# Routed rows of an expert layer: pads written once instead of cleared storage, one array for both parts, 20 + 19 tiles instead of 31 + 15, and a new order of the work

## The chip, the cores and the metric

The kernel runs on one core of a Trainium2 chip. The metric is device time in microseconds (us): the median of several executions, and one execution that the hardware profiler recorded. TensorE is called PE, VectorE DVE, ScalarE ACT, GpSimd POOL and SyncE SP, as in the profile.

## The reference

A batch is 128 rows of 128 numbers; there are 32 batches. Everything is float32.

```python
x = x + attn(layernorm(x))                       # 16 heads of 8, full 128x128 scores, w_out, x added again
x = x + xattn(layernorm(x), ctx, ctx)            # 16 heads of 64, rotary q and k, a row sees itself and 32 before it
# expert layer, on n = layernorm(x):
idx = argmax(n @ router.T)                       # one of 8 experts for each row
y  = (silu(n @ gate[idx].T) * (n @ up[idx].T)) @ down[idx].T
ys = (silu(n @ w_gate_s.T) * (n @ w_up_s.T)) @ w_down_s.T      # shared expert, all rows
x = x + n + y + ys
```

Which expert a row goes to is known only on the chip.

## The kernel before

Each engine runs a list of steps, written out by hand in one loop `for s in range(PERIODS)`. `batch(f, s - k)` runs step `f` for batch `s - k`, so a **period** `s` holds one batch of every step, each for another batch: `a_*` (norm, q/k/v), `b_*` (self attention), `c_v`, `r_k`, `r_q`, `d_*` (cross attention), `e_*`/`f_*` (router, shared expert, scatter). The order within a period, the lags `k`, and the table `BANK`, which puts every PE result into one of 8 PSUM banks, were fixed together. `take` makes PE wait until the last user of a bank has released it. `WARM` lists matmuls on ones that fill PE's waits in the first periods.

The routed expert is done afterwards, on rows that have been sorted by expert:

- `f_pos(b)`: PE counts rows by expert so far and gives each row of batch `b` its place in a DRAM array `z_xs`; DVE picks it (`psf`), POOL turns it into an integer. `f_send(b)` on POOL scatters the 128 rows (normed row, number of the row, and the sum to which the expert's result is added: 272 floats) with an indirect DMA.
- The batches are in two chunks, `CHUNKS = [24, 8]`, each with its own array. An expert's region has room for all rows of the chunk. So that unused rows of a tile do no harm, `clear(b)` on SP writes `fill` rows over the whole region, a part for each batch: one DMA of 8 x 128 rows, 1088 KB, in every period, and one more of the same size per chunk for a tile that belongs to nobody.
- After the last batch of a chunk DVE works out in `tile_table` which rows and which expert each of the chunk's tiles has: 24 + 7 = 31 tiles of 128 rows, and 8 + 7 = 15. This is the most that can be needed, since every expert's last tile may be part full.
- A tile: `load_r` (SP) loads 128 rows; `x_tr` (PE, line 399) turns them; `x_up` (410) gate and up; tanh on ACT, `x_gate` on DVE; `x_hT` (419); `x_dn` (425, 427); `x_y` adds on DVE; `x_send` (POOL, 1023) scatters the result to the output. `tile(f, s - k, i)` puts four tiles in each late period of the loop, for the first chunk only; the second chunk's tiles run after the loop (`last`).

PE's steps with the lines that the profile names: `b_s` 207, `b_nm` 216, `b_st` 224/228, `b_pv` 239, `c_v` 272, `r_k` 282, `r_q` 292, `d_s` 299/307, `d_t` 320, `d_pv` 334/337, `d_wo` 348, `f_up` 366, `f_pos` 385 to 389.

Of the kernel before, what the change touches and what calls it, by code (L numbers as in the profile page):

```python
# [13 lines left out]
NB = 32  # L14
# [3 lines left out]
CHUNKS = [24, 8]  # L18
TILES = [n + 7 for n in CHUNKS]
NT = sum(TILES)  # L20
# [10 lines left out]
BANK = dict(a=5, cnt=2, dn=5, ds0=0, ds1=3, ds2=1, ds3=4, dt0=1, dt1=4, dt2=2, dt3=4, et=5, gu=0, hi0=0, hi1=1, kE=7,  # L31
            kO=0, ln=1, lo0=6, lo1=4, nmt=5, oT=5, po=5, pos=6, qE=3, qO=7, qkv=6, rt=3, s0=6, s1=2, s2=5, s3=7,
            st0=6, st1=2, st2=5, st3=7, v0=3, v1=4, wo=2, x1=7, xg0=3, xg1=7, xg2=3, xg3=2, xgt0=1, xgt1=2, xgt2=3,
            xr0=5, xr1=0, xr2=5, xr3=6, xrt0=4, xrt1=5, xt0=1, xt1=6, xt2=7, xt3=2, xtt0=0, xy0=6, xy1=0, xy2=2,
            xy3=1, xyt0=6, xyt1=7)
WARM = {('a', 0): 36, ('nmt', 0): 43, ('st0', 0): 9, ('po', 0): 33, ('oT', 0): 13, ('qE', 0): 9, ('st0', 1): 16,
        ('ds0', 0): 14, ('oT', 1): 28, ('lo1', 0): 17}
S0, PERIODS = 24, 42


SEMS = """d_c1 d_cb d_c2 d_wk d_wv d_wq d_wo d_we d_ex d_tab
# [10 lines left out]
            d_x=3, d_cx=4, d_zf=4, d_ze=2, d_sc=4, d_xr=12, d_out=4)  # L52


def build(nc, A):
    ctx = ExitStack()
    with ctx:
# [13 lines left out]
        cb = sb("cb", [128, 1336], U16)  # L71
# [15 lines left out]
        cnt = sb("cnt", [128, 48])  # L87
        cmpb = sb("cmpb", [128, 8 * MOST])
        exf = sb("exf", [128, 2 * MOST])
# [46 lines left out]
        ecap = cb[:, 768:784].bitcast(BF16).rearrange("p (c e) -> p c e", c=2)  # L136
        far, eye = cb[:, 784:1296].bitcast(BF16).rearrange("p (w q) -> p w q", w=4), cb[:, 1296:1328].bitcast(BF16)
        iota = cb[:, 1328:1336].bitcast(BF16)
        woutT, bo, fill, tri = c2[:, 0:128], c2[:, 128:256], c2[:, 256:256 + ROW], c2[:, 528:592]
        tri = tri.rearrange("p (a b) -> p a b", a=8)  # L140
        rtT, ids = c2[:, 592:600], c2[:, 608:640].bitcast(U32)
# [31 lines left out]
        def _(pe):  # L173
# [205 lines left out]
            def f_pos(b):  # L379
                first = b == FIRST[chunk(b)]  # L380
                last = b + 1 in (FIRST[1], NB)
                p = take("pos", b, (S["v_cnt"], chunk(b) + 1) if last else (S["v_pse"], b + 1))
                pe.wait_ge(S["v_oh"], b + 1)
                pe.wait_ge(S["p_acc"], b + 1)
                pe.matmul(p[:, 0:8], ones[:, :], ecap[:, chunk(b), :], start=True, stop=False, skip_group_check=True)
                if not first:
# [43 lines left out]
            for s in range(PERIODS):  # L430
                batch(b_s, s - 3)
                tile(x_up, s - 31, 0)
                tile(x_dn, s - 32, 1)
                tile(x_hT, s - 32, 3)
                batch(c_v, s - 3, 1)
                batch(b_ln, s - 4)
                tile(x_dn, s - 32, 2)
                tile(x_tr, s - 31, 2)
                batch(d_pv, s - 5, 0)
                batch(r_q, s - 4, 0)  # L440
                batch(e_tr, s - 6)
                batch(r_q, s - 4, 1)
                batch(d_t, s - 5, 1)
                batch(b_nm, s - 3)
                tile(x_dn, s - 32, 3)
                batch(f_pos, s - 7)
                batch(f_up, s - 6)
                batch(d_pv, s - 5, 1)
                batch(b_st, s - 3)
                batch(d_s, s - 4)  # L450
                tile(x_hT, s - 31, 0)
                tile(x_tr, s - 31, 3)
                tile(x_up, s - 31, 1)
                batch(b_pv, s - 3)
                batch(d_wo, s - 5)
                batch(b_oT, s - 3)
                tile(x_dn, s - 31, 0)
                tile(x_up, s - 31, 2)
                batch(r_k, s - 2, 0)
                batch(a_qkv, s - 2)  # L460
                batch(b_cn, s - 3)
                batch(f_dn, s - 6)
                tile(x_tr, s - 30, 0)
                tile(x_hT, s - 31, 1)
                batch(c_v, s - 2, 0)
                batch(b_x1, s - 3)
                batch(a_tr, s - 1)
                tile(x_up, s - 31, 3)
                tile(x_tr, s - 30, 1)
                tile(x_hT, s - 31, 2)  # L470
                batch(r_k, s - 2, 1)
                batch(d_t, s - 4, 0)
# [7 lines left out]
        def _(dve):  # L480
# [148 lines left out]
            def f_pos(b):  # L629
# [6 lines left out]
                dve.tensor_reduce(f[:, 8:9], f[:, 0:8], AX.X, ALU.add).then_inc(S["v_pse"], 1)  # L636
                if b + 1 in (FIRST[1], NB):
                    dve.tensor_copy(cnt[:, 0:8], bank("pos")[:, 8:16]).then_inc(S["v_cnt"], 1)
                    tile_table(chunk(b))


            def tile_table(c):
                n, t0, T = CHUNKS[c], TILE0[c], TILES[c]
# [3 lines left out]
                                  steps[:, 0:n].rearrange("p (a j) -> p a j", a=1).to_broadcast([128, NE, n]),  # L647
                                  ALU.is_gt).then_inc(S["v_own"], 1)
                dve.wait_ge(S["v_own"], own())
                dve.tensor_reduce(cnt[:, 8:16], cm, AX.X, ALU.add).then_inc(S["v_own"], 1)  # L650
                c2 = cmpb[:, 0:64].rearrange("p (e f) -> p e f", e=NE)
                dve.wait_ge(S["v_own"], own())
                dve.tensor_tensor(c2, cnt[:, 8:16].rearrange("p (a f) -> p a f", a=1).to_broadcast([128, NE, NE]),
                                  tri[:, :, :], ALU.mult).then_inc(S["v_own"], 1)
                dve.wait_ge(S["v_own"], own())
                dve.tensor_reduce(cnt[:, 16:24], c2, AX.X, ALU.add).then_inc(S["v_own"], 1)
                c3 = cmpb[:, 0:8 * T].rearrange("p (j e) -> p j e", e=NE)
                dve.wait_ge(S["v_own"], own())
                dve.tensor_tensor(c3, cnt[:, 16:24].rearrange("p (a e) -> p a e", a=1).to_broadcast([128, T, NE]),
                                  tiles[:, 0:T].rearrange("p (j a) -> p j a", a=1).to_broadcast([128, T, NE]),  # L660
                                  ALU.is_le).then_inc(S["v_own"], 1)
                dve.wait_ge(S["v_own"], own())
                dve.tensor_reduce(exf[:, 0:T], c3, AX.X, ALU.add).then_inc(S["v_own"], 1)
                dve.tensor_scalar(cnt[:, 24:32], cnt[:, 8:16], -1.0, float(n), ALU.mult, ALU.add).then_inc(S["v_own"], 1)
# [3 lines left out]
                dve.tensor_tensor(c3, c3, cnt[:, 24:32].rearrange("p (a e) -> p a e", a=1).to_broadcast([128, T, NE]),  # L668
# [7 lines left out]
                dve.wait_ge(S["v_own"], own())  # L676
                dve.tensor_scalar(exr[:, t0:t0 + T], exf[:, MOST:MOST + T], 128.0, None, ALU.mult).then_inc(S["v_ex"], 1)
# [17 lines left out]
            for s in range(PERIODS):  # L695
                batch(d_ri, s - 6, 3)
                tile(x_gate, s - 33, 3)
                batch(r_k3, s - 4)
                batch(b_max, s - 4, 0)
                batch(b_max, s - 4, 3)  # L700
                batch(b_max, s - 4, 1)
                tile(x_y, s - 33, 1)
                tile(x_gate, s - 32, 0)
                batch(b_max, s - 4, 2)
                tile(x_y, s - 33, 2)
                batch(d_ox, s - 6, 0)
                batch(r_q1, s - 5)
                batch(r_q3, s - 5)
                batch(f_pos, s - 8)
                tile(x_y, s - 33, 3)  # L710
                batch(f_route, s - 7)
                batch(f_gate, s - 7)
                batch(d_ox, s - 6, 1)
                batch(d_max, s - 5, 1)
                batch(a_stats, s - 1)
                batch(d_max, s - 5, 3)
                batch(d_max, s - 5, 0)
                batch(d_ri, s - 5, 1)
# [18 lines left out]
        def _(act):  # L737
# [142 lines left out]
            for s in range(PERIODS):  # L880
                batch(b_ps, s - 5, 1)
                batch(b_ps, s - 5, 3)
                batch(b_ps, s - 5, 2)
                tile(x_hT, s - 33, 0)
                tile(x_xT, s - 33, 3)
                batch(d_exp, s - 6, 1)
                tile(x_th, s - 33, 1)
                batch(b_oT, s - 5)
                batch(d_exp, s - 6, 0)
                batch(d_exp, s - 6, 2)  # L890
                tile(x_th, s - 33, 2)
                batch(a_q, s - 4)
                batch(b_cnT, s - 5)
                batch(d_exp, s - 6, 3)
                batch(a_aT, s - 3)
                tile(x_xT, s - 32, 0)
# [168 lines left out]
        def _(sp):  # L1065
# [14 lines left out]
            def clear(b):  # L1080
                c, k = chunk(b), b - FIRST[chunk(b)]
                Z = A["z_xs"][c].rearrange("(t p) d -> p t d", p=128)
                if b == 0:
                    sp.wait_ge(S["d_c2"], 16)
# [129 lines left out]
```

## Time and profile before

| | us |
|---|---|
| median of 3 runs | 826.36 (820.38 to 828.25) |
| the profiled execution, device time | 820.7 |
| its span, first to last instruction | 818.7 |
| PE busy | 754.7 |
| DVE, ACT, POOL busy | 556.5, 542.3, 534.4 |

Busy time shows which engine has least room. A row of the timeline gives start, duration, engine, line, operation and, in brackets, the idle time just before it with what ended it. In the chain of waits "issue" stands where the engine waited for nothing that the profile shows.

### The profile page before, as it was taken

How to read it: one execution, taken by the hardware profiler on the slowest of the kernel's cores; microseconds unless marked ns; L12 is line 12 of the kernel's file. 1: busy time of each engine (PE TensorE's matmuls, PEld its weight loads, DVE VectorE, ACT ScalarE, POOL GpSimd, SP SyncE). 2: the span in 40 equal slices, each digit the busy share in tenths (PEclk: the TensorE clock that was granted, in tenths of full speed). 3: DMA queues.
4: the chain of work that ended last, by engine and by line, in shares of the span. 5: the costliest groups of instructions: out<-in, count | busy, mean ns of one | idle time of the engine just before them, and what ended most of it. 6: DMA issues, size and time to landing. Idle time of an engine off the chain costs nothing.

```text
span 818.7 us, 31875 instructions
## 1 busy us (share of the span) xinstructions
PE 754.7 (92%) x11894; PEld 615.7 (75%) x11894; DVE 556.5 (68%) x1414; ACT 542.3 (66%) x1964; POOL 534.4 (65%) x864
## 2 busy tenths in 40 slices
PE   6888999999999999989999999999869999999794
PEld 5666888887887888877787888888657778877453
DVE  3465777776777777756777777777677776665542
ACT  2366777776777777755777777777547677666242
POOL 4365677777667777766666777777546567676624
PEclk9999999999999999999999999999989999999888
DMA  6003122222222222222211122122134213321130
GB/s 228 10 12 111 64 90 91 92 90 83 89 90 90 70 71 70 70 70 70 70 64 68 67 75 70 67 75 85 53 121 146 67 48 91 103 87 59 42 109 13
DMA packets 56805, 64.29 MB, mean 79 GB/s; under 512 B 4014, under 2 KB 52916, under 8 KB 56656
## 3 DMA queue, kind: packets, MB, share of 16 engines
q1 hardware_dynamic: 52928, 54.06, 20.3%
q0 software_dynamic: 3008, 6.57, 2.3%
q8 instruction: 99, 1.62, 0.8%
q10 hardware_dynamic: 720, 1.63, 0.5%
q14 instruction: 50, 0.41, 0.2%
HBM read 17.80 MB, written 45.35 MB: 77 GB/s over the span
## 4 chain that ended last, share of the span: by engine, by line
PE 88%; issue 4%; DVE 3%; DMA 2%; ACT 1%; SPq 1%; POOL 0%; POOLq 0%; DVEq 0%; ACTq 0%
PE P L307 8%; PE P L348 8%; PE P L292 7%; PE P L272 7%; PE P L282 7%; PE P L320 5%; PE P L410 5%; PE P L334 4%; PE P L239 4%; PE P L224 4%; PE P L207 4%; PE P L366 4%; PE P L247 2%; PE P L337 2%; PE P L374 2%
## 5 line engine op out<-in xcount | busy, mean ns | idle before, releaser
L820 ACT ACTIVATE PX<-P,mx 128x128 f32<-128x128 f32 x512 | 183.1, 409 | 59.7 <-DVE mx L582 59.7
L582 DVE TENSOR_REDUCE mx<-P 128x4 f32<-128x512 f32 x128 | 83.1, 673 | 111.9 <-PE P L307 111.9
L990 POOL TENSOR_TENSOR PX<-PX,mx 128x512 f32<-128x512 f32 x128 | 131.9, 1040 | 3.6 <-DVE mx L587 2.6
L820 ACT ACTIVATION_READ_ACCUMULATOR PX<-P,mx 128x1 f32 x512 | 128.0, 250 | 0.0
L829 ACT ACTIVATE PT<-P 128x512 f32<-128x512 f32 x128 | 69.6, 596 | 45.2 <-PE P L320 44.5
L985 POOL TENSOR_TENSOR rq<-rq,tq 128x1024 f32<-128x1024 f32 x32 | 75.4, 2358 | 34.5 <-DVE tq L546 34.5
L307 PE MATMUL P<-rk,rq 32*128 32x128 f32 x2048 | 73.7, 286 | 18.2 <-issue 18.1
L936 POOL TENSOR_SCALAR st<-st 128x1 f32<-128x1 f32 x96 | 22.0, 229 | 103.4 <-DVE st L490 100.3
L521 DVE TENSOR_REDUCE nmf<-P 128x4 f32<-128x512 f32 x128 | 79.8, 683 | 13.7 <-PE P L207 13.7
L307 PEld LDWEIGHTS P<-rk,rq 32*128 32x128 f32 x2048 | 66.9, 196 | 20.2 <-issue 20.0
L784 ACT ACTIVATE PS<-P 128x512 f32<-128x512 f32 x128 | 66.1, 603 | 22.7 <-PE P L228 22.7
L980 POOL TENSOR_TENSOR rk<-rk,tk 128x1024 f32<-128x1024 f32 x32 | 75.6, 2363 | 0.9
L272 PE MATMUL P<-wvT,cxT 128*128 128x512 f32 x128 | 68.9, 620 | 0.1
L292 PE MATMUL P<-cT,wq 128*128 128x128 f32 x512 | 68.9, 281 | 0.0
L282 PE MATMUL P<-cxT,wk 128*128 128x128 f32 x512 | 68.6, 277 | 0.0
L1023 POOL DMA_INDIRECT out<-yst,xrow x46 | 45.8, 995 | 34.4 <-DVE yst L692 22.2
L348 PE MATMUL P<-woT,oX 128*128 128x128 f32 x512 | 65.6, 281 | 0.0
L348 PEld LDWEIGHTS P<-woT,oX 128*128 128x128 f32 x512 | 59.6, 191 | 7.4 <-issue 6.1
L292 PEld LDWEIGHTS P<-cT,wq 128*128 128x128 f32 x512 | 61.9, 191 | 3.7
L282 PEld LDWEIGHTS P<-cxT,wk 128*128 128x128 f32 x512 | 63.2, 194 | 1.8 <-issue 1.7
L938 POOL TENSOR_TENSOR st<-st,nhalf 128x1 f32<-128x1 f32 x96 | 54.6, 569 | 8.0
L334 PE MATMUL P<-PT,V 64*64 64x96 f32 x1024 | 56.2, 249 | 0.0
(148 smaller groups left out, 1884.9 us busy)
## 6 DMA issues: line engine op xcount, KB each, us to landing
z_xs<-c SPq DMA_DIRECT2D x34, 1088.0 KB, 5.1
xrow<-z_xs SPq DMA_DIRECT2D x46, 136.0 KB, 2.1
ew<-in_ew SPq DMA_DIRECT2D x9, 384.0 KB, 3.4
x<-in_x SPq DMA_DIRECT2D x32, 64.0 KB, 1.9
cxT<-in_ctxT SPq DMA_DIRECT2D x31, 64.0 KB, 1.8
out<-yst,xrow POOLq DMA_INDIRECT x46, 2.2
wk<-in_wk SPq DMA_DIRECT2D x1, 512.0 KB, 4.2
wvT<-in_wvT SPq DMA_DIRECT2D x1, 512.0 KB, 6.9
```

The source lines that it names most:

```text
L272: pe.matmul(p, cxT[b % 4][:, :], wvT[:, 4 * half:4 * half + 4, :].rearrange("p a n -> p (a n)"), start=True, stop=True).then_inc(S[f"t_v{h ...
L282: t = pe.matmul(p[:, c * 128:c * 128 + 128], wk[:, e, c, :], cxT[b % 4][:, :], start=True, stop=True)
L292: t = pe.matmul(p[:, c * 128:c * 128 + 128], wq[:, e, c, :], cT[b % 2][:, :], start=True, stop=True)
L307: t = pe.matmul(p[r][:, c * 128:c * 128 + 128], rq[b % 2][32 * r:32 * r + 32, e, c, :], rk[b % 2][32 * r:32 * r + 32, e, c, :], start=Fals ...
L334: pe.matmul(lo[64 * u:64 * u + 64, 96 * q:96 * q + 96], V[b % 3][0:64, 8 * k + 2 * q + u, :], PT[(2 * b + k) % 3][0:64, 2 * q + u, 0:96], ...
L348: t = pe.matmul(p[:, 0:128], oX[2 * (b % 2) + k][:, q, :], woT[:, 4 * k + q, :], start=(k == 0 and q == 0), stop=(k == 1 and q == 3))
L521: dve.tensor_reduce(nmf[b % 2][:, 0, r, :], v3(bank(f"s{r}")), AX.X, ALU.max, negate=True).then_inc(S["v_bm"][r], 1)
L582: dve.tensor_reduce(mx[b % 3][:, 0, r, :], v3(bank(f"ds{r}")), AX.X, ALU.max, negate=True).then_inc(S["v_dm"][r], 1)
L820: t = act.activation(PX[(4 * b + r) % 6][:, c, :], p[:, c * 128:c * 128 + 128], ACT.Exp, bias=m[:, 0, r, c:c + 1], scale=1.0, accum_out=m[ ...
L980: pool.tensor_tensor(rk[b % 2][:, :, :, :], rk[b % 2][:, :, :, :], tk[:, :, :, :], ALU.add).then_inc(S["p_k"], 1)
L985: pool.tensor_tensor(rq[b % 2][:, :, :, :], rq[b % 2][:, :, :, :], tq[:, :, :, :], ALU.add).then_inc(S["p_q"], 1)
L990: pool.tensor_tensor(X[:, :, :], X[:, :, :], mx[b % 3][:, 2, r, :].rearrange("p (h a) -> p h a", a=1).to_broadcast([128, 4, 128]), ALU.mul ...
```

## The change

Both chunks now share one array `z_xs` with `CAP = 33` tiles of room for each expert. Chunks are 27 and 5 batches. At the first table only **full** tiles are taken: 27 batches hold at least 20 of them whatever the routing, so `TILES[0] = 27 - 7 = 20`; what is over stays in the array for the second table, which takes the rest of 39: 19 tiles. The running counts are no longer restarted at the second chunk. A part full tile exists only at the end of each expert's rows, so `clear` is gone. `pads`, once, when batch 30 is counted, writes 256 `fill` rows behind the rows counted so far for each of the 8 experts (8 DMAs of 272 KB, each at an address that SP loads from `padr`); the scatter of batch 31 waits for them (`d_pad`). `nobody` writes 8 tiles of 136 KB, one in each of periods 18 to 25.

Orders, lags, `BANK` and `WARM` (218 matmuls before, 185 now) are all new. Tiles start in period 35 instead of 30, `PERIODS` is 45 instead of 42.

```diff
-CHUNKS = [24, 8]
-TILES = [n + 7 for n in CHUNKS]
-NT = sum(TILES)
+CHUNKS = [27, NB - 27]
+CAP = NB + 1
+NT = NB + 7
+TILES = [CHUNKS[0] - 7, NT - CHUNKS[0] + 7]
...
 # DVE, f_pos
+                if b == NB - 2:
+                    dve.scalar_tensor_tensor(out=padr[:, :], in0=experts, scalar=float(128 * CAP), in1=bank("pos")[:, 8:16],
+                                             op0=ALU.mult, op1=ALU.add).then_inc(S["v_pad"], 1)
...
 # DVE, tile_table
+                if c == 1:
+                    dve.tensor_tensor(own_tiles, own_tiles, done, ALU.subtract).then_inc(S["v_own"], 1)
...
+                if c == 0:
+                    dve.memset(cnt[:, 40:41], 0.0).then_inc(S["v_own"], 1)
+                    dve.tensor_scalar(upto, incl, float(T), None, ALU.min).then_inc(S["v_own"], 1)
...
+                    dve.tensor_tensor(done, upto, before, ALU.subtract).then_inc(S["v_own"], 1)
+                else:
+                    dve.tensor_tensor(w, w, after, ALU.add).then_inc(S["v_own"], 1)
...
+                    dve.tensor_tensor(w, w, done, ALU.subtract).then_inc(S["v_own"], 1)
...
 # POOL, f_send
-                pool.wait_ge(S["d_zf"][b % 4], 16 * (b // 4 + 1))
+                if b == NB - 1:
+                    pool.wait_ge(S["d_pad"], 16 * NE)
...
 # SP
-            def clear(b):
...
-                sp.dma_start(Z[:, k:NE * CHUNKS[c]:CHUNKS[c], :], fill[:, :].rearrange(
-                    "p (a d) -> p a d", a=1).to_broadcast([128, NE, ROW])).then_inc(S["d_zf"][b % 4], 16)
+            def pads(b):
+                if b == NB - 2:
+                    sp.wait_ge(S["v_pad"], 1)
+                    for e in range(NE):
+                        row = sp.value_load(padr[0:1, e:e + 1], min_val=128 * CAP * e, max_val=128 * (CAP * e + CAP - 2))
+                        sp.dma_start(A["z_xs"][bass.ds(row, 256), :].rearrange("(t p) d -> p t d", p=128),
+                                     empty.to_broadcast([128, 2, ROW])).then_inc(S["d_pad"], 16)
+            def nobody(s):
+                e = s - 18
+                if 0 <= e < NE:
+                    k = 128 * (NE * CAP + e)
+                    sp.dma_start(A["z_xs"][k:k + 128, :], fill).then_inc(S["d_ze"], 16)
...
 # the order, two lines of each kind
-                batch(f_pos, s - 8)
...
+                batch(f_pos, s - 7)
...
-                tile(x_up, s - 31, 0)
...
+                tile(x_up, s - 35, 0)
```

Four places show how instructions moved. First SP, in two periods near the end of the first chunk; `z_xs<-c` is a clear, `cxT` and `x` are the loads of a batch.

```order
97 L1090 DMA z_xs<-c 128x8x272
98 L1077 DMA cxT<-in_ctxT 128x128
99 L1069 DMA x<-in_x 128x128
100 L1086 DMA z_xs<-c 128x8x272
101 L1090 DMA z_xs<-c 128x8x272
```

Now there is nothing between the loads; the pads (L1122, L1123, eight such groups) stand once, behind tile loads (L1148, L1149).

```order
157 L1148 TENSOR_LOAD exr
158 L1148 ISA x2
159 L1149 ISA
160 L1149 DMA xrow<-z_xs 128x272
161 L1122 TENSOR_LOAD padr
162 L1122 ISA x2
163 L1123 ISA
164 L1123 DMA z_xs<-c 128x2x272
```

The large DMA in each period is gone, and one train of eight smaller ones has come near the end.

Second DVE, the end of the first table. `lg`, `OH` and `th` are the router and shared expert of the period, `oX` the step that releases a bank to `d_s` on PE.

```order
874 L672 TENSOR_SCALAR exg<-exf 128x31
875 L673 TENSOR_REDUCE exf<-cmpb 128x31
876 L675 TENSOR_TENSOR exf<-exf,c 128x31
877 L677 TENSOR_SCALAR exr<-exf 128x31
878 L608 MAX lg<-P 128x8
879 L610 MAX_INDEX lgu<-lg,P 128x8
880 L612 TENSOR_TENSOR OH<-P,lgu 128x8
881 L618 SCALAR_TENSOR_TENSOR th<-th,P 128x256
882 L621 SCALAR_TENSOR_TENSOR th<-th,P 128x256
```

And now, where `xab` and `st_3` are the sum and statistics behind the self attention, `tk` a rotary product, `nmf` the maxima of scores:

```order
963 L705 TENSOR_SCALAR exg<-exf 128x20
964 L706 TENSOR_REDUCE exf<-cmpb 128x20
965 L708 TENSOR_TENSOR exf<-exf,c 128x20
966 L714 TENSOR_SCALAR exr<-exf 128x20
967 L547 TENSOR_TENSOR xab<-P,xab 128x128
968 L496 BN_STATS st_3<-xab 128x6
969 L498 BN_AGGR st_3<-st_3 128x2
970 L595 RECIPROCAL mx<-mx 128x4
971 L554 TENSOR_TENSOR tk<-P,tab 128x1024
```

The table moved from ahead of the router to ahead of the last steps of the period.

Third POOL, in a steady period: `nmf`/`nm` make the 4 instructions of `b_nm`, for which PE waits at line 216; `rq` and `rk` are the rotary sums that `d_s` needs.

```order
578 L950 CAST nm<-nmf 128x4x4
579 L952 TENSOR_TENSOR nmf<-nmf,nm 128x16
580 L954 CAST nm<-nmf 128x4x4
581 L956 TENSOR_TENSOR nm<-nmf,nm 128x4x4
582 L971 TENSOR_TENSOR xab<-x,arow 128x128
583 L975 TENSOR_TENSOR xab<-xab,c 128x128
584 L985 TENSOR_TENSOR rq<-rq,tq 128x1024
585 L1004 CAST pos<-psf 128x1
586 L1012 COPY er<-c 128x1
587 L1018 DMA z_xs<-er,pos 25600x272
588 L980 TENSOR_TENSOR rk<-rk,tk 128x1024
```

Now:

```order
555 L1027 TENSOR_TENSOR PX<-PX,mx 128x512 x2
556 L1017 TENSOR_TENSOR rk<-rk,tk 128x1024
557 L987 CAST nm<-nmf 128x4x4
558 L989 TENSOR_TENSOR nmf<-nmf,nm 128x16
559 L991 CAST nm<-nmf 128x4x4
560 L993 TENSOR_TENSOR nm<-nmf,nm 128x4x4
561 L1041 CAST pos<-psf 128x1
562 L1022 TENSOR_TENSOR rq<-rq,tq 128x1024
563 L1048 COPY er<-c 128x1
564 L1055 DMA z_xs<-er,pos 34816x272
```

The sum of `rk` moved ahead of `b_nm`, `xab` behind the scatter.

Fourth POOL, at the scatter of the last batch:

```order
801 L1000 TENSOR_TENSOR acc<-acc,OH 128x8
802 L1023 DMA out<-yst,xrow 4096x128 x3
803 L1004 CAST pos<-psf 128x1
804 L1023 DMA out<-yst,xrow 4096x128
805 L1012 COPY er<-c 128x1
806 L1018 DMA z_xs<-er,pos 9216x272
807 L1023 DMA out<-yst,xrow 4096x128 x18
```

And now, up to the same scatter (L1055):

```order
754 L1037 TENSOR_TENSOR acc<-acc,OH 128x8
755 L1060 DMA out<-yst,xrow 4096x128
756 L1041 CAST pos<-psf 128x1
757 L1048 COPY er<-c 128x1
758 L1055 DMA z_xs<-er,pos 34816x272
759 L1060 DMA out<-yst,xrow 4096x128 x28
```

The output scatter that stood between the position and the last scatter of rows has moved behind the latter. On PE, behind the counting matmuls of batch 31, two `x_up` of the loop are left before, and six now.

## Rows read from the trace of the kernel before

**Rows 1.** The page: the clock granted to PE in 40 slices, in tenths.

```profile
PEclk9999999999999999999999999999989999999888
```

**Rows 2.** The chain of waits in order of time: start, us, what.

```profile
172.66 1.98 PE P L348 x16
...
190.66 1.93 issue
...
194.99 1.98 PE P L348 x16
...
494.37 1.98 PE P L348 x16
...
514.58 1.98 PE P L348 x16
...
580.43 1.99 PE P L348 x16
```

**Rows 3.** PE's waits, longest in total: us, times, longest.

```profile
PE P L307 <- issue: 18.1, 9, 3.6
PE P L299 <- DVE oX L593: 8.9, 2, 7.6
PE P L399 <- DMA xrow<-z_xs: 4.0, 2, 3.3
...
PE P L419 <- DVE xth L685: 3.0, 3, 2.1
```

**Rows 4.** Timeline: PE at the first pause, SP's clear of one period.

```profile
69.76 0.50 PE L307 MATMUL P<-rk,rq 32*128 32x128 f32 x6 [2.93 <-issue]
...
185.68 0.43 SPq L1090 DMA_DIRECT2D z_xs<-c  x1
```

**Rows 5.** Busy us of PE, PEld, DVE, ACT, POOL in 1 us; clock, DMA share, GB/s.

```profile
188.00:189.00 1.00, 1.00 (x39) 1.00 (x42) 0.86 (x3) 0.66 (x2) 1.00 (x2) 1.00 1.05 363
...
191.00:192.00 1.00, 0.00 (x0) 0.00 (x0) 0.00 (x0) 0.43 (x1) 0.97 (x2) 1.00 0.38 139
```

**Rows 6.** The page: queue of instructions (packets, MB, share), and the clears' issues.

```profile
q8 instruction: 99, 1.62, 0.8%
...
z_xs<-c SPq DMA_DIRECT2D x34, 1088.0 KB, 5.1
```

**Rows 7.** Timeline of POOL: the scatter of rows in the same period.

```profile
189.94 1.11 POOL L1018 DMA_INDIRECT z_xs<-er,pos  x1 [0.66 <-POOL er L1012]
```

**Rows 8.** The chain, two periods with four tiles each.

```profile
660.05 1.98 PE P L348 x16
...
686.75 1.98 PE P L348 x16
```

**Rows 9.** Timeline of PE after the loop: two tiles' first matmuls.

```profile
795.54 0.27 PE L399 MATMUL P<-c,xrow 128*128 128x128 f32 x1
...
797.17 0.27 PE L399 MATMUL P<-c,xrow 128*128 128x128 f32 x1
```

**Rows 10.** Timeline at the first table: three of DVE's steps, and POOL beside.

```profile
594.68 2.34 DVE L646 TENSOR_TENSOR cmpb<-cnt,c 128x192 f32<-128x192 f32 x1
...
598.73 2.65 DVE L664 TENSOR_SCALAR cnt<-cnt 128x8 f32<-128x8 f32 x1
...
602.70 0.18 DVE L677 TENSOR_SCALAR exr<-exf 128x31 uint32<-128x31 f32 x1
...
594.45 2.36 POOL L985 TENSOR_TENSOR rq<-rq,tq 128x1024 f32<-128x1024 f32 x1 [0.85 <-DVE tq L546]
```

**Rows 11.** Timeline at the second table: DVE's last step, POOL's last scatter of rows.

```profile
769.58 0.17 DVE L677 TENSOR_SCALAR exr<-exf 128x15 uint32<-128x15 f32 x1
...
772.19 0.98 POOL L1018 DMA_INDIRECT z_xs<-er,pos  x1 [0.28 <-POOL er L1012]
```

**Rows 12.** Columns as in Rows 5, 5 us behind the second table.

```profile
780.00:785.00 5.00, 5.00 (x9) 2.22 (x10) 1.62 (x4) 1.49 (x5) 0.00 (x0) 0.50 0.51 136
```

**Rows 13.** The page: the sum of `rk` on POOL.

```profile
L980 POOL TENSOR_TENSOR rk<-rk,tk 128x1024 f32<-128x1024 f32 x32 | 75.6, 2363 | 0.9
```

More of the change, by code:

```diff
@@ L379, in f_pos @@
             def f_pos(b):
[L380 to L382 removed]
+                until = [(S["v_pse"], b + 1)]
+                if b == NB - 2:
+                    until.append((S["v_pad"], 1))
+                if b + 1 in (FIRST[1], NB):
+                    until.append((S["v_cnt"], chunk(b) + 1))
+                p = take("pos", b, *until)
                 pe.wait_ge(S["v_oh"], b + 1)
                 pe.wait_ge(S["p_acc"], b + 1)
[L385 to L386 removed]
+                pe.matmul(p[:, 0:8], ones[:, :], ecap, start=True, stop=False, skip_group_check=True)
+                if b:
                     pe.matmul(p[:, 0:8], ones[:, :], acc[:, b, :], start=False, stop=False, skip_group_check=True)
@@ L444, in _ @@
[L444 to L471, printed above, removed]
@@ L472, in _ @@
-                batch(d_t, s - 4, 0)
+                batch(c_v, s - 4, 1)
+                tile(x_tr, s - 35, 0)
+                tile(x_up, s - 36, 3)
+                tile(x_hT, s - 36, 1)
+                tile(x_dn, s - 36, 0)
+                batch(b_ln, s - 5)
+                batch(d_pv, s - 6, 0)
+                batch(e_tr, s - 7)
+                batch(r_q, s - 5, 1)
+                tile(x_hT, s - 36, 2)
+                batch(r_q, s - 5, 0)
+                batch(d_t, s - 6, 1)
+                tile(x_dn, s - 36, 1)
@@ new lines, in _ @@
+                batch(f_up, s - 7)
+                batch(b_nm, s - 4)
+                batch(d_pv, s - 6, 1)
+                batch(a_tr, s - 2)
+                tile(x_tr, s - 35, 1)
+                batch(b_st, s - 4)
+                tile(x_dn, s - 36, 2)
+                batch(d_s, s - 5)
+                batch(r_k, s - 3, 0)
+                batch(b_pv, s - 4)
+                tile(x_hT, s - 36, 3)
+                tile(x_up, s - 35, 0)
+                tile(x_tr, s - 35, 2)
+                batch(f_dn, s - 7)
@@ new lines, in _ @@
+                batch(a_qkv, s - 3)
+                batch(b_oT, s - 4)
+                batch(d_wo, s - 6)
+                batch(b_cn, s - 4)
+                tile(x_up, s - 35, 1)
+                tile(x_dn, s - 36, 3)
+                batch(f_pos, s - 7)
+                batch(c_v, s - 3, 0)
+                tile(x_tr, s - 35, 3)
+                batch(b_x1, s - 4)
+                batch(r_k, s - 3, 1)
+                tile(x_up, s - 35, 2)
+                batch(d_t, s - 5, 0)
+                batch(b_s, s - 3)
@@ L473, in _ @@
+                tile(x_hT, s - 35, 0)
             for j in range(TILE0[1], NT + 4):
@@ L1140, in _ @@
                 weights(s)
-                tile(next_r, s - 34, 0)
+                nobody(s)
+                tile(next_r, s - 36, 0)
+                tile(next_r, s - 36, 1)
+                tile(next_r, s - 36, 2)
                 batch(next_x, s - 3)
-                batch(clear, s - 6)
-                tile(next_r, s - 34, 1)
-                batch(first_r, s - 8)
-                tile(next_r, s - 34, 2)
-                tile(next_r, s - 34, 3)
+                tile(next_r, s - 37, 3)
+                batch(pads, s - 7)
                 batch(next_cx, s - 3)
+                batch(first_r, s - 7)
             for j in range(TILE0[1], NT):
```

228 lines of the change are left out of this document (112 added, 116 removed).

## The prediction

> **What bounds the kernel.** I read the timeline by windows first. From 460 to 560 us every engine but PE is idle a quarter of the time, and the chain of waits is there an unbroken run of PE instructions: the output projection of one batch starts at 494.37 and that of the next at 514.58 [rows 2]. So a quiet period is 20.21 us of PE work, and nothing else costs. The page's clock line is full almost everywhere [rows 1]. Then I looked for periods that are longer. Between the projections at 172.66 and 580.43 lie 19 periods, 407.8 us; at 20.21 each they would be 384.0. So 23.8 us are lost there. The chain names the loss: pieces called "issue", in which PE has work and no wait that the profile shows, such as the one from 190.66 to 192.59 [rows 2]. Last I read PE's list of waits [rows 3]: "issue" at line 307, 18.1 us in nine pauses; DVE's `oX`, 7.6 at once, at the first tile table; waits for tiles' rows and hidden values, 4.0 and 3.0, round the second table.
>
> **What the pauses are.** SP issues a clear at 185.68 [rows 4]. It keeps the DMA engines at a share of 1.05 and 363 GB/s from 188 to 189, and PE stops at 190.66, while DVE and PE both stand still from 191 to 192 [rows 5]. A clear is 1088 KB and takes 5.1 us to land; the instructions themselves come over a queue too, 99 packets and 1.62 MB, so 16 KB each [rows 6]. I found ten pauses of over 1 us in the loop's first 600 us, each a few tenths to 3 us behind the landing of a clear, and the longest, 3.6 us [rows 3], behind the two clears that are issued together at the second chunk. My reading: a block of instructions has to wait behind the clear, and PE runs dry when the block falls due early in a clear. Periods in which it falls due elsewhere are quiet, clears or not, and so the losses come in groups.
>
> [...]
>
> **The change part by part.** The sum is made against the profiled execution, 820.7 us (span 818.7 and 2.0 around it).
>
> - **Seven tiles fewer.** Two periods with four tiles in them: 26.70 us from projection to projection [rows 8], 6.49 more than the quiet one, 1.62 a tile. Behind the loop a tile takes 1.63, from 795.54 to 797.17 [rows 9]. PE is full in both places, so it doesn't matter that 11 tiles leave the loop and 4 join the end: 46 - 39 = 7 tiles at 1.63 are **-11.4**.
> - **No clears in the loop.** All 23.8 us go, if nothing takes the clears' place. The loads of a batch (64 KB each) and the tiles of `nobody` (136 KB) are an eighth of a clear or less, and the scatter of rows is there already in quiet periods. The pause of 2.93 at 69.76 [rows 4], behind the two clears at the start of the first chunk, goes as well: **-26.7**. Bounds: 0, and 26.7 plus the first pauses of DVE and ACT, which cost nothing of their own.
> - **First table.** The table holds DVE from 594.68 to 602.88 [rows 10], 8.2 us, and PE waits 7.6 of them [rows 3] for `oX`, queued behind. Two of its steps are long, 2.34 and 2.65, and ordinary ones are 0.18 [rows 10] to 0.4; the first ends as POOL's rotary sum ends (594.45 + 2.36 = 596.81, DVE at 597.02). Without both it is 3.7, and the new one has three small steps more, fewer columns for 20 tiles and more for 27 batches: 4.2. In the new place POOL's next work, the reciprocal root behind `st_3`, itself waits for DVE, so I expect POOL idle beside most of the table. Queued behind the table are now `xab`, `tk` and the four maxima, and PE needs each of them within half a microsecond of when it is due, so it waits about 4. That is **-4**, between 0 (held by POOL as before) and -7.
> - **The end.** Behind the count of batch 31 the old kernel has little work: it waits 2.7 of the 3.0 for DVE in the second table, then 4.0 for rows [rows 3], since the last scatter starts only at 772.19, 2.6 us behind the table [rows 11], after an output scatter that had to wait for the table. Then the clock is down: 0.50 from 780 to 785 with PE busy throughout [rows 12], which alone loses 2.5, some 4 in all. Now six `x_up` of the loop are left, about 9 us of PE work, and the scatter stands ahead of the outputs: the 4.0 go. The table is longer (16 steps to 13, rows of 256): 4.3 for 3.0, and the tiles' `x_gate` is still behind it: PE waits 4 for 2.7. Clock: 2 lost for 4. Together -4.0 + 1.3 - 2.0, **-5** rounded.
> - **Pads.** 2.2 MB, twice a clear, so 10.2 us from the row of a clear [rows 6]; they start when batch 30 is counted, and the scatter of batch 31 would be due some 10 to 12 later. Bounds: 0 (hidden), and 3.6 (a pause as behind the double clear [rows 3]) plus 5 (scatter late, and behind it on POOL the outputs of tiles, for whose buffers DVE and SP wait). Eight DMAs of 272 KB leave gaps in which a block of instructions can pass: I take **+2**. `nobody` and the 33 warm-up matmuls fewer: 0, hidden by PE's waits for the first batch.
> - **The new order.** PE's steps are the same and nearly in the same cyclic order, the list merely starts elsewhere. I walked one period with the durations of a quiet one: cross-attention maxima, exponentials, normalisation, `d_t` keep the 7.7 us that they have; the sum of `rk` (2.36 [rows 13]) is now ahead of `b_nm` on POOL, for which PE waits, but `f_up` has moved ahead of that transpose and gives 1.3, and POOL has a hole of 1.3 there. I find no step late, but a dozen that are early by only 0.1 to 0.7. Bounds 0 to 0.5 a period; I take **+2** for the loop.
>
> [...]
>
> **Sum.** -11.4 - 26.7 - 4 - 5 + 2 + 2 = -43.1; 820.7 - 43.1 = 777.6. The median shown is 5.7 above the profiled execution; part of that spread should be the pauses, whose phase varies, so I add little: **778**.
>
> **Rivals.**
> - *The pauses are not the clears'.* POOL's scatter is issued at 189.94 [rows 7], 0.7 before PE stops, and lands about when PE goes on. If its descriptors or rows hold the instructions up, all pauses stay: 777.6 + 26.7 = **804**. For it: the place in the period. Against it: the scatter is as large and as near in quiet periods, and the longest pause is where clears, not scatters, are doubled. [...] 0.10.
> - *The order is a little late in each period*, 0.5 us by one of the tight slots, in 32 periods: 16, **794**. 0.10.
> - *Pads in the way*: the full 8.6, and as much again in clock and refilling: some 15 for 2, **791**. 0.07.
> - *Slower: POOL becomes the bound.* The sum of `rk` ahead of `b_nm` delays the transpose of maxima, the scores and all behind. If none of its 2.36 us fits into a hole, PE waits 2.36 in 31 periods, 73 us: 777.6 + 73 = **851**. It passes the kernel before by 1% from 1.7 us a period on. Against it: POOL works 534 of 819 us, so it has 7 us of room per period, and the hole is where the sum goes. 0.04.
> - *It does not do what it says*: the 20 tiles of the loop can hold no pads, and the code fixes the number of tiles at 39, so the tiles go in any case. The clears go too. Nothing left here.
>
> **How the numbers follow.** My case has 0.69; its own range, with table and end at their bounds and 0 to 0.3 a period for the order, is 766 to 788. With 794 and 791 in, 0.86 lies between 764 and 799, and I give 764 to 799; the scatter's 804 and the 851 are outside. A measurement of this kernel tells about 1%, 8 us, from no change: faster by more, all cases but POOL's and half of what I have not thought of, 0.93; within it 0.03; slower 0.04.
>
> **What will show it.** Projections 20.2 us apart from 100 us to the first table, with no "issue" at line 307: right on the clears. Pauses of 1 to 3 us behind scatters: the first rival. A period of 20.7 or 22.6 with PE waiting for `nm` or `oX`: the order. At the first table a PE wait of 4 instead of 7.6, with no step of 2.3. Behind the last count one PE wait of about 4 for DVE and none for `xrow`; a wait there for rows, with POOL's last scatter late, would be the pads. Tiles 1.63 apart at the end, 19 of them. Should the time be wrong by more than 15, it will be because one of the short slacks that I walked was misjudged, or a clear slowed more than these pauses.

## The result, and the profile after

The changed kernel takes **773.82 us** (median of 4 runs, 772.18 to 774.75); the kernel before takes 825.7 on the same chip. The ratio is 0.9377, with a 95% interval of 0.9328 to 0.9427. The profiled execution took 773.4, with a span of 771.3: 47.4 less than the span before.

The chain of waits gives the periods, as [rows 2] before: start, us, what. The row from `L353` is now the output projection.

```profile
65.21 1.79 PE P L353 x16
...
126.60 1.79 PE P L353 x16
147.82 1.79 PE P L353 x16
...
310.15 1.79 PE P L353 x16
331.63 1.79 PE P L353 x16
...
393.43 1.79 PE P L353 x16
413.62 1.79 PE P L353 x16
...
617.05 1.80 PE P L353 x16
643.02 1.79 PE P L353 x16
```

A quiet period is 20.19 us (393.43 to 413.62). Some are still longer: 21.2 from 126.60, 21.5 from 310.15. The 27 periods from 65.21 to 617.05 are 551.8 us, 6.7 more than 27 quiet ones. The same sum for the 24 periods before, from the first projection at 71.27 to the one at 580.43 [rows 2], is 24.1.

PE's waits, against [rows 3]:

```profile
PE P L427 <- DVE xth L722: 4.0, 3, 3.3
PE P L212 <- DVE xab L547: 2.9, 1, 2.9
PE P L312 <- issue: 2.7, 5, 0.8
```

"issue" at `d_s` (now line 312) has gone from 18.1 us to 2.7, the wait of 7.6 for `oX` has become one of 2.9 for `xab`, and none for `xrow` is left. One of the pauses that remain, and PE behind the first table, on the timeline (start, us, engine, line; idle time before in brackets):

```profile
618.89 1.10 PE L277 MATMUL P<-wvT,cxT 128*128 128x512 f32 x2
...
324.47 1.10 PE L312 MATMUL P<-rk,rq 32*128 32x128 f32 x26
326.39 1.39 PE L312 MATMUL P<-rk,rq 32*128 32x128 f32 x38 [0.82 <-issue]
...
624.70 2.09 PE L212 MATMUL P<-KM,qT 32*128 32x512 f32 x8 [2.95 <-DVE xab L547]
626.72 2.08 PE L277 MATMUL P<-wvT,cxT 128*128 128x512 f32 x2
```

DVE's table, against [rows 10], and POOL beside it:

```profile
620.57 0.38 DVE L663 TENSOR_TENSOR cmpb<-cnt,c 128x216 f32<-128x216 f32 x1
...
622.24 0.17 DVE L686 TENSOR_SCALAR cnt<-cnt 128x8 f32<-128x8 f32 x1
...
623.96 0.18 DVE L714 TENSOR_SCALAR exr<-exf 128x20 uint32<-128x20 f32 x1
...
624.97 0.22 POOL L973 TENSOR_SCALAR st<-st 128x1 f32<-128x1 f32 x1 [3.88 <-DVE st L498]
```

Neither the first step (2.34 before) nor the one on `cnt` (2.65 before) is held: the table takes 3.6 us, and POOL is idle for 3.88. The period costs 5.8 over the quiet one all the same, for a wait of 2.95: behind the wait PE is slower, two matmuls of line 277 take 2.08 where they took 1.10 before the table, and the clock, 1.00 up to 624, is 0.50 from 626 to 628 and 0.83 over 620 to 640. With POOL idle no step of the table is over 0.38 us; an experiment below brings the two long ones back (2.37 and 3.04), beside rotary sums of POOL.

The end of the program, against [rows 11] and [rows 12]: PE behind the last count (its four matmuls stand at 708.24), SP's pads, the last scatter of rows, and five us in the columns of [rows 5].

```profile
701.70 9.49 SPq L1123 DMA_DIRECT2D z_xs<-c  x8
...
714.10 0.66 PE L427 MATMUL P<-c,xth 128*128 128x128 f32 x2 [3.32 <-DVE xth L722]
...
713.83 0.98 POOL L1055 DMA_INDIRECT z_xs<-er,pos  x1 [4.26 <-DMA z_xs<-c]
...
715.00:720.00 5.00, 5.00 (x20) 4.00 (x20) 1.62 (x5) 1.55 (x6) 3.64 (x4) 0.54 0.39 118
```

PE waits once, 3.32 us, for `x_gate` behind the second table. The scatter stands 4.26 us for the pads and nobody notices: PE has rows in hand until it lands. The clock is 0.54 over the stretch shown, 715 to 720, behind the wait; it is 1.00 over 705 to 710 and over 720 to 725.

### The profile page after: what moved, and what is told of

Read it like the earlier page. It is cut to its first block, busy times and chain, and to the rows that moved or that the text cites. A ratio compares the mean times of both kernels' runs of the same rounds, so it can differ in the third digit from the quotient of the medians.

```text
span 771.3 us, 31550 instructions
## 1 busy us (share of the span) xinstructions
PE 740.5 (96%) x11799; PEld 603.4 (78%) x11799; DVE 544.2 (71%) x1401; ACT 534.7 (69%) x1943; POOL 525.7 (68%) x857
## 3 DMA queue, kind: packets, MB, share of 16 engines
q10 hardware_dynamic: 720, 1.63, 0.6%
## 4 chain that ended last, share of the span: by engine, by line
PE 91%; DVE 2%; ACT 2%; issue 2%; DMA 1%; SPq 0%; POOL 0%; POOLq 0%; ACTq 0%; DVEq 0%
PE P L277 8%; PE P L312 8%; PE P L287 8%; PE P L297 7%; PE P L353 7%; PE P L339 6%; PE P L325 5%; PE P L229 5%; PE P L212 4%; PE P L371 4%; PE P L244 4%; PE P L418 4%; PE P L379 3%; PE P L252 2%; PE P L342 1%
## 5 line engine op out<-in xcount | busy, mean ns | idle before, releaser
L590 DVE TENSOR_REDUCE mx<-P 128x4 f32<-128x512 f32 x128 | 81.2, 678 | 93.5 <-PE P L312 93.5
L857 ACT ACTIVATION_READ_ACCUMULATOR PX<-P,mx 128x1 f32 x512 | 119.3, 233 | 0.0
L277 PE MATMUL P<-wvT,cxT 128*128 128x512 f32 x128 | 72.2, 646 | 0.0
L287 PE MATMUL P<-cxT,wk 128*128 128x128 f32 x512 | 71.6, 283 | 0.0
L312 PE MATMUL P<-rk,rq 32*128 32x128 f32 x2048 | 68.2, 275 | 2.9 <-issue 2.7
L312 PEld LDWEIGHTS P<-rk,rq 32*128 32x128 f32 x2048 | 62.2, 187 | 4.6 <-issue 4.4
L297 PE MATMUL P<-cT,wq 128*128 128x128 f32 x512 | 63.1, 276 | 0.0
L353 PE MATMUL P<-woT,oX 128*128 128x128 f32 x512 | 62.4, 275 | 0.0
L339 PEld LDWEIGHTS P<-PT,V 64*64 64x64 f32 x1024 | 45.5, 134 | 18.6 <-issue 18.1
L353 PEld LDWEIGHTS P<-woT,oX 128*128 128x128 f32 x512 | 59.7, 192 | 0.0
```

The lines of the kernel that those rows point to most:

```text
L277: pe.matmul(p, cxT[b % 4][:, :], wvT[:, 4 * half:4 * half + 4, :].rearrange("p a n -> p (a n)"), start=True, stop=True).then_inc(S[f"t_v{h ...
L287: t = pe.matmul(p[:, c * 128:c * 128 + 128], wk[:, e, c, :], cxT[b % 4][:, :], start=True, stop=True)
L297: t = pe.matmul(p[:, c * 128:c * 128 + 128], wq[:, e, c, :], cT[b % 2][:, :], start=True, stop=True)
L312: t = pe.matmul(p[r][:, c * 128:c * 128 + 128], rq[b % 2][32 * r:32 * r + 32, e, c, :], rk[b % 2][32 * r:32 * r + 32, e, c, :], start=Fals ...
L339: pe.matmul(lo[64 * u:64 * u + 64, 96 * q:96 * q + 96], V[b % 3][0:64, 8 * k + 2 * q + u, :], PT[(2 * b + k) % 3][0:64, 2 * q + u, 0:96], ...
L353: t = pe.matmul(p[:, 0:128], oX[2 * (b % 2) + k][:, q, :], woT[:, 4 * k + q, :], start=(k == 0 and q == 0), stop=(k == 1 and q == 3))
```

## The experiments

They ran on three chips, in three sets; each set has its own runs of the kernel before, and ratios are against those. Set 2 is a chip like that of the result, "the first chip" below (before: 824.23 us). On the chips of sets 1 and 3 the same kernel takes 865.72 and 869.21. The changed kernel itself ran in sets 2 and 3, and no profile of the kernel before was taken in sets 1 and 3. The two kernels again, unedited:

> The changed kernel again, as the measure for the others of this set and, if the chip is the slower one of the first set (865.7 us for the kernel before), for those too. If the chip only has more and longer pauses at instruction blocks and clears, the changed kernel is hardly slower there than 773.8: under 785, a ratio under 0.92. If the chip slows the scores' matmuls beside every scatter, as the 21.2 us periods of the run with clears put back suggest, it has 21 us periods without any clear: some 800 us.

770.9 us, ratio 0.9353 (0.9328 to 0.9378), set 2.

> The kernel before once more, with a profile on this chip. On a chip where it takes 826: groups of long periods as in its first profile. On one where it takes 866: either more of the pauses behind clears, some 60 us of them, or every period 1 us longer at the scores' matmuls (32 us) and the rest in pauses.

826.89 us, one execution, set 2. "issue" at `d_s` is 19.7 us in 10 pauses, and the chain has the long periods in groups again (lines of the projection, and the pauses ahead of them):

```profile
176.38 2.27 issue
...
183.05 1.98 PE P L348 x16
...
201.14 1.84 issue
...
205.38 1.98 PE P L348 x16
...
270.58 1.98 PE P L348 x16
...
290.80 1.98 PE P L348 x16
```

22.3 us for one period, 20.2 for another, as in the first profile, and the long ones stand at much the same places: the pauses belong to the kernel. Its first projection is at 76.07, though, 4.8 later than in the first profile.

> The changed kernel as the measure for this set. Where the kernel before takes 825: 769 to 775. On a chip like the first set's: by the periods of 21.2 us seen there, 795 to 800 if the chip slows the scores without clears too, 775 to 785 if the clears do it.

805.38 us, ratio 0.9252 (0.9177 to 0.9327), set 3. The ratio is much the same, but nearly each period is 21.2 us, with no clear anywhere. It is `d_s`:

```profile
100.90 2.14 PE L312 MATMUL P<-rk,rq 32*128 32x128 f32 x64 [0.72 <-issue]
...
312.15 1.11 POOL L1055 DMA_INDIRECT z_xs<-er,pos  x1 [0.29 <-POOL er L1048]
...
312.25 3.06 PE L312 MATMUL P<-rk,rq 32*128 32x128 f32 x64
```

64 matmuls in 3.06 us, beside POOL's issue of the scatter, at a clock of 1.00 and with DVE idle. The scatters begin at 99.92: up to the `d_s` at 100.90 the 64 take 2.0 to 2.1 us on this chip too, and from the next one on 2.8 to 3.3. On the first chip, with a scatter in the same place:

```profile
407.65 1.11 POOL L1055 DMA_INDIRECT z_xs<-er,pos  x1 [0.29 <-POOL er L1048]
...
407.76 2.02 PE L312 MATMUL P<-rk,rq 32*128 32x128 f32 x64
```

### Data flow without the order

All of the change but the order: tables, pads, 20 and 19 tiles as changed; order, `BANK` and `WARM` of before, with the pads fitted in and the tiles three periods later. Up to the first table its lists of batch steps are those of before, less the clears.

```diff
             for s in range(PERIODS):       # PE; the other engines likewise
-                batch(c_v, s - 4, 1)
-                tile(x_tr, s - 35, 0)
+                batch(b_s, s - 3)
+                tile(x_up, s - 34, 0)
...
                 batch(next_x, s - 3)       # SP
+                batch(pads, s - 8)
+                tile(next_r, s - 37, 1)
```

> The new data (one array, 20 + 19 tiles, pads, no clears) in the old order: the old lists of steps, lags, banks and warm-up matmuls, with the tiles three periods later, since the first chunk has 27 batches. By the sum on record the order gives the first table (4 us), the end (5) and takes 2: this kernel should be 5 to 9 us slower than the changed one, with a wait of 4 to 8 us for oX at the first table and one for rows behind the last count. Rival (the order gives nothing): the same time within 2 us. Rival (the order gives most of the gain): over 15 us slower.

794.29 us, ratio 0.9626 (0.9598 to 0.9653), set 2. So the data flow is worth 29.9 us and the order **23.4** more (794.3 to 770.9), against the 5 to 9 that I gave it; the rival with over 15 came out. The chain and the timeline say where. PE and DVE:

```profile
71.53 1.98 PE P L353 x16
...
618.46 1.98 PE P L353 x16
...
648.25 1.98 PE P L353 x16
...
632.70 2.37 DVE L663 TENSOR_TENSOR cmpb<-cnt,c 128x216 f32<-128x216 f32 x1
...
636.39 3.04 DVE L686 TENSOR_SCALAR cnt<-cnt 128x8 f32<-128x8 f32 x1
...
632.47 2.35 POOL L1022 TENSOR_TENSOR rq<-rq,tq 128x1024 f32<-128x1024 f32 x1 [0.84 <-DVE tq L554]
...
637.05 2.35 POOL L1017 TENSOR_TENSOR rk<-rk,tk 128x1024 f32<-128x1024 f32 x1
...
716.11 8.98 SPq L1123 DMA_DIRECT2D z_xs<-c  x8
...
728.10 0.45 PE L407 MATMUL P<-c,xrow 128*128 128x128 f32 x1 [7.68 <-DMA xrow<-z_xs]
```

- *The loop.* 27 periods take 546.9 us, 1.8 more than quiet ones: all the long ones are gone, in an order in which [rows 3] has 18.1 us of pauses and the control of this set 19.7. In this stretch the clears are what was taken out. With the new order the same stretch takes 550.9 (64.68 to 615.56): the new order costs 4.0 here.
- *The start.* The first projection is at 71.53, against 64.68: 6.9. In the old order PE waits 3.2 for DVE's `vpad`, 2.6 in two for ACT's `oT` and 2.2 for its `PS` up to then; in the new one no wait is over 1.2.
- *The first table.* Both long steps are back, and each ends with a rotary sum of POOL: 632.47 + 2.35 = 634.82 for 635.07, and 637.05 + 2.35 = 639.40 for 639.43. The period is 29.8 us, against 24.7: 5.1.
- *The end.* Behind the table the old order takes 144.3 us and the new one 127.7 (640.26 to 768.0): 16.6. The largest single piece is 7.68: PE waits for the rows of a tile whose load is queued on SP behind the 8.98 us of pads. In the new order the tiles that PE reaches meanwhile have been loaded ahead of the pads. With two shorter ones the waits for rows are 9.7. Part of the rest is the clock: 0.82 over 640 to 660 and 0.88 over 750 to 790, against 1.00 and, over 720 to 765, 0.95 in the new order.

6.9 - 4.0 + 5.1 + 16.6 = 24.6, the difference of the two spans (792.6 and 768.0).

### The clears put back, whole and in eight

Into a spare array, from SP, behind the load of `x` as before. The kernel `e_clear_2` is `e_clear` again, in set 3.

```diff
+            def clear(b):
+                Z = A["z_dum"][b % 4].rearrange("(t p) d -> p t d", p=128)
...
+                for i in range(1):         # e_clear8: range(8)
+                    n = NE // 1            # e_clear8: NE // 8
+                    sp.dma_start(Z[:, n * i:n * i + n, :], fill[:, :].rearrange(
+                        "p (a d) -> p a d", a=1).to_broadcast([128, n, ROW])).then_inc(S["d_zf"][b % 4], 16)
...
                 batch(next_x, s - 3)
+                batch(clear, s - 6)
```

> The changed kernel with the clearing put back as traffic alone: in each of 32 periods SP issues one DMA of 1088 KB of fill rows, at its old place in the period, into four scratch arrays that nothing reads. My theory (a block of instructions waits behind a clear): pauses called issue at the matmuls of the cross-attention scores come back in groups, 10 or so of 1 to 3 us, and 20 to 27 us in all: 795 to 801 us. Rival (the pauses come from the scatter of rows, or from the old order): no more than 3 us are added, 774 to 777. Second rival (PE is also slowed a little in every period by the traffic): a quiet period longer than 20.2 us.

804.43 us, ratio 0.9277 (0.9240 to 0.9315), set 1.

> As the run with the clears put back, but each as 8 DMAs of 136 KB, one after another: the same bytes, at nearly the same time. If a block of instructions can pass between two DMAs, few or short pauses come back: 775 to 782 us. If what counts is the traffic as such, it is as long as with whole clears, 795 to 801.

804.48 us, ratio 0.9286 (0.9253 to 0.9319), set 1.

> The changed kernel with one clear of 1088 KB in each period again (traffic alone, into scratch arrays), now with the changed kernel itself in the same set. Where the kernel before takes some 825 us: pauses of 1 to 3 us in groups, 15 to 25 us more than the changed kernel, 786 to 796. If instead the new order is not hurt by clears, as nearly 771. On a chip like the first set's (866 before): about 804, and the changed kernel tells whether its 21.2 us periods come from the clears.

806.2 us, ratio 0.9267 (0.9193 to 0.9340), set 3: 0.8 more than the changed kernel beside it (805.38), and no difference that its interval can tell. My expectation failed. In the new order 32 clears of 1088 KB cost nothing in set 3, and in set 1, where the changed kernel itself did not run, one piece and eight take the same time. Clears in flight are thus not enough for a pause. The place of a clear against `d_s` isn't that of before, though. SP's clear in the new order:

```profile
318.30 0.44 SPq L1141 DMA_DIRECT2D z_dum<-c  x1
...
332.98 0.97 PE L312 MATMUL P<-rk,rq 32*128 32x128 f32 x13
```

It starts 14.7 us ahead of `d_s` and has landed (4.9 us from issue) long before it; in the kernel before it was issued 5.0 us ahead of the pause at `d_s` (185.68 to 190.66, [rows 2, 4]). A clear right ahead of `d_s` in the new order, and the clears on the first chip, were not tried.

### The kernel before, with its clears in eight

```diff
-                sp.dma_start(Z[:, k:NE * CHUNKS[c]:CHUNKS[c], :], fill[:, :].rearrange(
-                    "p (a d) -> p a d", a=1).to_broadcast([128, NE, ROW])).then_inc(S["d_zf"][b % 4], 16)
+                for i in range(NE):
+                    k0 = k + i * CHUNKS[c]
+                    sp.dma_start(Z[:, k0:k0 + 1, :], fill[:, :].rearrange(
+                        "p (a d) -> p a d", a=1)).then_inc(S["d_zf"][b % 4], 16)
```

> The kernel before with each clear issued as 8 DMAs of 136 KB to the same rows, nothing else changed. My theory, if instructions can pass between DMAs: most of the 23.8 us of long periods go, 800 to 812 us. If the bytes count and not their grouping: 820 to 828, as before. A third way: SP needs 8 issues of some 0.4 us, and its loads of batches come later; they are three batches ahead, so this costs nothing.

838.16 us, ratio 0.9653 (0.9596 to 0.9711), set 1.

> The kernel before with each clear as 8 DMAs of 136 KB again. In the first set it was 0.965 of the kernel before. If a block of instructions passes between the pieces, the groups of long periods are gone or short, and it is 10 to 24 us faster than the kernel before on any chip. If only that chip profits: 820 to 826.

836.9 us, ratio 0.9635 (0.9555 to 0.9716), set 3. PE's waits there, and a clear with the `d_s` beside it:

```profile
PE P L299 <- DVE oX L593: 7.6, 1, 7.6
PE P L307 <- issue: 6.1, 21, 0.9
...
290.04 5.46 SPq L1094 DMA_DIRECT2D z_xs<-c  x8
...
293.88 1.58 PE L307 MATMUL P<-rk,rq 32*128 32x128 f32 x48
295.65 0.76 PE L307 MATMUL P<-rk,rq 32*128 32x128 f32 x16 [0.18 <-issue]
```

The same bytes, at the same place in the same order, and 28 to 32 us less; no pause at `d_s` is over 0.9 us, where the kernel before, on the first chip, has them up to 3.6 [rows 3]. Periods are 20.4 to 20.7 us mostly. So neither the number of bytes nor the scatter, which is as it was, made what went. But cutting the clear also spreads it: its issue takes SP 4.8 to 5.5 us instead of 0.43, and beside the one issued at 208.08 in set 3 the DMA engines move at most 291 GB/s in a microsecond, at a share of 0.87, where a whole clear has 363 at 1.05 [rows 5]. Whether the size of one DMA hurts or the rate at which the clear runs wasn't tested.

The two profiles of set 3 show one thing more: `d_s` takes some 2.5 us beside a scatter in this old order, and 3.05 in the new one. On this chip a period of the loop is 20.6 us here and 21.2 in the changed kernel, which has no clears at all. The new order's cost in the loop, 4.0 us in set 2, is thus more like 16 there (0.6 in each of 27 periods); the old order without clears was not run on such a chip.

### The scatter twice

```diff
+                pool.indirect_dma_start(out=A["z_dum"], out_offset=bass.IndirectOffsetOnAxis(ap=pos[:, b:b + 1], axis=0),
+                                        in_=er[b % 4][:, :], in_offset=None).then_inc(S["d_sc"][b % 4], 16)
```

> The changed kernel with every scatter of 128 rows made twice, the second into a scratch array. Rival (the scatter's descriptors and rows hold up the instructions): pauses at the cross-attention scores come back, 10 us or more in all. My theory: no pauses; POOL is 1.1 to 1.4 us longer in each period in front of work with a slack of a few tenths, so at most 0 to 1 us a period in waits for POOL, 774 to 800 us, and the waits named are POOL's, not issue.

870.12 us, ratio 1.0060 (1.0017 to 1.0103), set 1; the changed kernel with clears takes 804.43 there, so a second scatter costs 66 us, 2 a period. I had expected 0 to 26 for it, in waits for POOL and not in pauses. Periods are 22.1 to 23.9 us. PE in one of them, and the two scatters:

```profile
260.27 1.11 POOL L1055 DMA_INDIRECT z_xs<-er,pos  x1 [0.29 <-POOL er L1048]
261.69 0.96 POOL L1057 DMA_INDIRECT z_dum<-er,pos  x1 [0.30 <-issue]
...
260.38 0.96 PE L312 MATMUL P<-rk,rq 32*128 32x128 f32 x13
261.57 0.53 PE L312 MATMUL P<-rk,rq 32*128 32x128 f32 x5 [0.23 <-issue]
262.28 0.52 PE L312 MATMUL P<-rk,rq 32*128 32x128 f32 x4 [0.18 <-issue]
263.02 2.03 PE L312 MATMUL P<-rk,rq 32*128 32x128 f32 x42 [0.22 <-issue]
```

22 matmuls take 2.6 us with their pauses beside the scatters, and the 42 behind them take 2.03. The clock is 1.00 from 260.3 to 263, where the 22 are, and 0.70 over 263 to 265. On these chips the scatter does slow PE, as the first rival had it, in small pieces and in every period; over 60 to 600 us the clock is 0.96, against 1.00 in `e_clear`, and what of the 66 us is the clock was not taken apart.

### Seven tiles more

`NT = NB + 14`; the last seven tiles hold no rows, and are computed.

```diff
-NT = NB + 7
+NT = NB + 14
```

> The changed kernel with 7 tiles more at the end, 39 + 7 = 46 as before: they load rows that belong to nobody and send nothing. By 1.63 us a tile it takes 11.4 us more than the changed kernel. If the end of the kernel were bound by loads or scatters and not by PE, a tile would cost another time than 1.63: 1.1 us by SP's issue, 1.3 by POOL's.

820.01 us, ratio 0.9422 (0.9346 to 0.9498), set 3: 14.6 more than 805.38, 13.7 by the spans. Tiles stand 1.63 apart on the timeline, so 11.4 of it is the tiles; the other 2 to 3 is within what the runs of each kernel differ by (801 to 807, 816 to 821).

### The waits at the tables filled

Matmuls on ones in PE's two waits: 38 at the first table, 42 at the second.

```diff
-        ('cnt', 1): 19, ('nmt', 2): 16}
+        ('cnt', 1): 19, ('nmt', 2): 16, ('s0', 30): 38}
...
+                if j == 13:
+                    for _ in range(42):
+                        pe.matmul(p[:, 384:512], ones[:, :], ones[:, :], start=True, stop=True, skip_group_check=True)
```

> The changed kernel with matmuls on ones in the two places where PE waits for DVE's tables: 38 ahead of the scores of batch 30 and 42 ahead of one turn of a hidden tile, with nothing else changed. The wait at the first table is 2.95 us but its period is 5.8 us longer than a quiet one, and behind the second the clock is 0.54: if the clock's fall is what costs the rest, filling the waits gives 3 to 6 us. If not, or if the fillers end later than the wait, 0 or a loss of up to 1 us.

769.7 us, ratio 0.9336 (0.9312 to 0.9360), set 2, against 770.9. I expected 3 to 6 us from it. Behind the first table the clock is held: 1.00 over 617 to 637 where the control has 0.91, and the two matmuls of line 277 take 1.13 us, where 2.08 stood in the first profile. The period of the table goes from 24.7 us to 23.3, but everything behind it takes 127.7 us in both kernels. The intervals overlap, and if there is a gain, it is 1 to 2 us: the clock behind these waits is worth less than I put on it.

```profile
623.63 1.14 PE L212 MATMUL P<-KM,qT 32*128 32x512 f32 x8 [0.57 <-issue]
624.70 1.13 PE L277 MATMUL P<-wvT,cxT 128*128 128x512 f32 x2
```

## Why the prediction was right

778 was forecast and 773.8 measured. Against the profiled executions the sum was -43.1, and -47.4 came out. By the prediction's terms, in spans on the first chip:

| | forecast | measured | from |
|---|---|---|---|
| seven tiles | -11.4 | -11.4 (-13.7 to -14.6 with spread) | 1.63 apart; seven tiles more |
| clears in the loop, and order there | -23.8 + 2 | -17.4 | 24.1 over quiet before, 6.7 after |
| start | -2.9 + 0 | -6.1 | first projection 71.27, now 65.21 |
| first table | -4 | -2.9 | 28.93 over the period of the table before, 25.97 after |
| end, pads | -5 + 2 | -9.6 | what is left |

**Clears.** That the pauses came with the clears was right and, with the old order, so was the size: data flow alone takes the loop from 24 us over quiet to 1.8 and the start 4.5 us forward (76.07 in the control, 71.53), where the forecast had 26.7. The start is weak evidence, since two profiles of the kernel before have it 4.8 apart. That the clears' form counts and not their bytes is shown by their splitting, on two chips (28 and 32 us). That it is a block of instructions that waits for a clear is still argued, and as I wrote it (a pause whenever a block falls due early in a clear) it is too simple: in the new order the same clears bring none. The trace of the kernel before has a packet of the instruction queue [rows 6] at the pause shown: it starts between 190.3 and 190.4, where the clear's traffic is nearly over (12 packets, 0.01 MB, of its queue from 190 to 190.5), and PE stops at 190.66. That PE waits for such a packet, and that one passes in the gap between two smaller DMAs, are estimates of mine; no run singles them out. What the traces show is the length: in the changed kernel, which has no clears, the pauses at `d_s` are 0.8 at most (1.0 in set 2), and in the kernel before up to 3.6 [rows 3].

**The new order in the loop.** I had +2 for slots that come late. It costs 4.0, and not by those: PE's longest waits name no `nm` or `oX` in the loop. The cost is pauses without a releaser and slower matmuls at `d_s`, up to 1.3 us in a period, in groups. On the chips of sets 1 and 3 nearly every period has 1.0 of it, beside the scatter. The first rival thus named something real, but it is not the cause of the long pauses before, which went with the clears while every scatter stayed.

**Start.** I gave warm-up and new order 0, "hidden by PE's waits for the first batch". The first projection is 6.1 us earlier. I had put that down to the pause of 2.9 alone; the order by itself, with no clears on either side, gives 6.9 in set 2. This term was missing.

**First table.** Right in kind, PE waits 2.9 where 4 was forecast and the table takes 3.6 for 4.2. But I took the gain from the waits alone: around a wait of 2.95 the period loses 5.8.

**End.** The steps came as written: one long wait for DVE (3.3 for 4), none for rows, a shorter stretch at a low clock. The pads, forecast at 2 with bounds 0 and 8.6, cost nothing that a row shows. About 4 us of this term I can't put down to rows. The upper bound is real: in the old order, with the pads ahead of a tile's load, PE waits 7.68.

**Where the errors met.** I credited the data flow with some 36 us and the order with 7. They are worth 29.9 and 23.4 in set 2: in the old order the data flow brings its own new wait at the end, and the order is what avoids it. Total and direction were right; the split was not, and that the total came within 4 us is in part luck: a loop that gave 4 less than forecast and a start and an end that gave 10 more.

**Still open**: why two of three chips slow `d_s` beside a scatter in every period, and more in the new order than in the old; whether the longer periods left on the first chip are the same thing; and whether clears hurt in the old order and not in the new one because of their place against `d_s`, which the runs agree with but don't single out.

## What to carry to other kernels

A single DMA of 1088 KB in each period went here with pauses of up to 3.6 us in an engine that waited for nothing; the profile calls them "issue", and on two chips cutting the DMA in eight gave 3.5% with nothing else changed (ratios 0.9653 and 0.9635). Cost a data-flow change and a reordering apart, by running the one without the other: here the order was worth nearly as much as the data, because it put a burst of writes behind a load that PE needed (a wait of 7.68 us otherwise), and a chain of small DVE steps where POOL was idle (3.6 us in the changed kernel; in the old order two of the steps alone take 2.37 and 3.04). A term "hidden, 0" at the start of a program needs the row that hides it, like any other.

## What the hardware showed that I had not expected

- One kernel takes 824 us on one chip and 866 to 869 on two others; the changed one 771 and 805. In the changed kernel 1.0 us a period of that is in 64 small matmuls beside a scatter that POOL issues: 3.06 us for 2.02, at a clock of 1.00. Before the first scatter the slower chip takes 2.0 to 2.1 as well.
- A second scatter there costs another 2 us a period, 66 in all, while its issue takes POOL 0.96.
- 1088 KB in one DMA and in eight differ by 28 to 32 us over 32 periods in one order, and by nothing in another, where the clear has landed before the 64 small matmuls start.
